# A graph network layer on one core: destinations broadcast instead of one-hot transposes, groups joined into sets, and one gathered tile of 25 copied column by column on ScalarE

## The chip, the cores and the metric

One core of a Trainium2 chip runs the whole program. The metric is the device time of one execution in microseconds, the median of three runs. A profile comes from one more execution; its times are measured from its first instruction.

## What is computed

Cut to what matters:

```python
h = relu(layernorm(x))                       # 12500 nodes x 128
s, d = src, dst                              # 400000 edges, sorted by dst
m = relu(concat([h[s], h[d], edge_attr]) @ w1 + b1) @ w2 + b2
agg = segment_sum(m, d, num_segments=12500)
# GRU cell: gates from agg @ w_ih + b_ih and h @ w_hh + b_hh
x_new = x + (1 - z) * n + z * h
```

The product with `w1` splits in three: `h[s] @ w1[0:128]` (called p), `h[d] @ w1[128:256]` (called q), and the edge attributes by the last 32 rows.

## The kernel before

**Setup.** The nodes are normalised in 14 batches; `hT` keeps h transposed in on-chip memory (128 features on the partitions, one node per column), and p is written to DRAM as `p_rows`, one row of 128 floats per node.

**Edges.** The 400000 edges are cut in 125 chunks of G = 5 groups of T = 5 tiles of P = 128 edges, so 25 tiles a chunk. `over_chunks` writes chunks 0 to 3 out, loops over the next ones and writes the last out again. Five engines run the same sequence, each with its own waits on semaphores.

- **GpSimd (POOL)** gathers `p_rows[src]` into `rows`, one indirect DMA for each tile (L423). It may overwrite a group's rows when `seg_ready` says that this group's sums of the chunk before are done.
- **VectorE (DVE)** builds the one-hot matrix of each tile's destinations against a window of W = 95 nodes (`build_onehot`, L790, 5 instructions a group), adds the products to the gathered rows (`add_pre`, L800), and adds the window sums to `acc` (`add_segments`, L809 and L810).
- **TensorE (PE)** transposes the one-hots (L1005), multiplies the window's features by `w1[128:256]` (L1008), forms q plus the edge part for five tiles (`pre_activation`, L1019), and sums messages per window node (`segment_sums`, L1032 and L1033).
- **ScalarE (ACT)** loads the window's base into a register (L563), copies the window's columns of `hT` to `h_win` (L568), copies the transposed one-hots to `lhs` with a count (`copy_onehot`, L574) and q to `rhs` (L575), and applies the ReLU to the rows (L580). Per chunk it also does the gate functions of 100 nodes (L592, L597) and issues a load and a store (L585, L601).
- **SyncE (SP)** loads indices and edge attributes.

The order on each engine is the order in which the code is written, shifted by groups with `before(c, s, back)`. The last chunk is followed by `finish_last`, which does the last 200 nodes' gates.

A group's step on ScalarE, for instance:

```python
copy_onehot(c, s)
if s + 1 < G:
    copy_window(c, s + 1)
old = before(c, s, 2)
if old:
    relu_message(*old)
```

Of the kernel before, what the change touches and what calls it, by code (L numbers as in the profile page):

```python
# [20 lines left out]
DST_PARTS = LOADS_AHEAD + 1  # L21
# [24 lines left out]
IOTA_PARTS = 5  # L46
assert W % IOTA_PARTS == 0

# [5 lines left out]

D = 128
# [3 lines left out]

def gnn_kernel(nc, x, src_cols, dst_cols, dst_rows, src_tiles, dst_tiles, ea_t, w1, b1, w2, b2, w_ih, b_ih, w_hh, b_hh, out):  # L60
    p_rows = nc.dram_tensor("p_rows", [NPAD, D], F32, kind="Internal").ap()
    base_f_dram = nc.dram_tensor("base_f_dram", [CHUNKS, G], F32, kind="Internal").ap()
    base_i_dram = nc.dram_tensor("base_i_dram", [CHUNKS, G], I32, kind="Internal").ap()
# [4 lines left out]
    with ExitStack() as ctx:  # L68
# [6 lines left out]
        def sems(name, n):  # L75
# [27 lines left out]
        base_i = low[ED:ED + 1, at:at + GROUPS].bitcast(I32)  # L103
        at += GROUPS
        assert at <= NPAD

        dst_int = sb("dst_int", [P, GROUPS * T], I32)
        dst_rel = dst_int[:, :].bitcast(F32)
        rows = sb("rows", [P, G, T, D])
        onehot = sb("onehot", [P, G, T, WB])  # L110
        base_bc = onehot[:, :, :, :].rearrange("p g t w -> p (g t w)")[:, 0:GROUPS]
        lhs = sb("lhs", [P, G, GE])
        rhs = sb("rhs", [P, G, D])
        h_win = sb("h_win", [P, W])
        w1_dst = sb("w1_dst", [P, D])
        idx = sb("idx", [P, G, T], I32)
        count = sb("count", [WB, G])
        ident = sb("ident", [P, P])
        iota_w = sb("iota_w", [P, IOTA_PARTS, W // IOTA_PARTS + 1])
# [15 lines left out]
        gmin = sb("gmin", [P, G])  # L135
        gmax = sb("gmax", [P, G])
        base_f = sb("base_f", [P, G])
        base_n = sb("base_n", [P, G], I32)
# [24 lines left out]
        g_b1, g_one = rhs[0:1, 0, :], lhs[0:1, 0, 0:P]  # L163
# [7 lines left out]
        onehotT_ps = ps[0:WB, 0:GE]  # L171
# [6 lines left out]
        q_ps = ps[0:W, GE:GE + D]  # L178
# [25 lines left out]
        dst_rel_ready, ones_set, acc_zeroed, deg_zeroed = (sem(n) for n in ("dst_rel_ready", "ones_set", "acc_zeroed", "deg_zeroed"))  # L204
        idx_in, ea_in, rows_in, h_win_ready = (sems(n, G) for n in ("idx_in", "ea_in", "rows_in", "h_win_ready"))
        onehot_ready, onehotT_ready, lhs_ready, pre_ready = (sems(n, G) for n in ("onehot_ready", "onehotT_ready", "lhs_ready", "pre_ready"))
        summed, message_ready, seg_ready, acc_added = (sems(n, G) for n in ("summed", "message_ready", "seg_ready", "acc_added"))
# [3 lines left out]
        fin_chain = sem("fin_chain")  # L211

# [3 lines left out]
        g_src_in, g_dst_in, g_ea_in = (sem(n) for n in ("g_src_in", "g_dst_in", "g_ea_in"))  # L216
        g_gathered = sems("g_gathered", 3)
        g_bc_ready, g_bcT_ready, g_pre_ready, g_summed, g_message_ready, g_seg_ready, g_new_ready = (sem(n) for n in (
            "g_bc_ready", "g_bcT_ready", "g_pre_ready", "g_summed", "g_message_ready", "g_seg_ready", "g_new_ready"))
# [14 lines left out]

        def over_chunks(eng, body, first=0):
            for c in range(first, LAG + 2):
                body(c)
            with eng.Fori(LAG + 2, CHUNKS) as c:  # L238
                body(c)


        def finishing(c):
            known = isinstance(c, int)
            return (c - LAG if not known or c >= LAG else None, c - LAG - 1 if not known or c > LAG else None)
# [17 lines left out]
        def _(sp):  # L262
# [24 lines left out]
            sp.dma_start(rhs[WB:P, :, :], w1[2 * D:2 * D + ED, :].unsqueeze(1).to_broadcast([ED, G, D])).then_inc(weights_in, 16)  # L287
            sp.dma_start(rhs[W:WB, :, :], b1.unsqueeze(0).unsqueeze(0).to_broadcast([1, G, D])).then_inc(weights_in, 16)
# [4 lines left out]
            sp.dma_start(dst_nat, dst_rows).then_inc(dstn_in, 16)  # L293
            turns = BATCHES // 2 - LOADS_AHEAD
# [14 lines left out]
            def load_indices(c, s):  # L309

                wait(sp, rows_in[s], c * (16 * T))
                sp.dma_start(idx[:, s, :], src_cols[bass.ds(c * (G * P) + s * P, P), :]).then_inc(idx_in[s], 16)
# [3 lines left out]

            part = GROUPS * T // DST_PARTS
            assert part * DST_PARTS == GROUPS * T

            def load_dst(k):  # L320
                sp.dma_start(dst_int[:, bass.ds(k * part, part)], dst_cols[:, bass.ds(k * part, part)]).then_inc(dst_in, 16)

            load_dst(0)
            with sp.Fori(turns, BATCHES // 2) as i:
                for par in range(2):
                    store(i, par)
                load_dst(i - (turns - 1))

            def load_group(c, s):

                if not (isinstance(c, int) and c == 0):
                    load_indices(c, s)

                wait(sp, pre_ready[s], c)
                sp.dma_start(lhs[WB:P, s, :], ea_t[:, bass.ds(c * (G * GE) + s * GE, GE)]).then_inc(ea_in[s], 16)

            def chunk(c):
                for s in range(G):
                    load_group(c, s)
                if isinstance(c, int) and c == 0:  # L340

                    sp.wait_ge(acc_zeroed, 2)
                    for par in range(2):
                        sp.wait_ge(p_stored[par], BATCHES // 2 * 16)
                        sp.wait_ge(hT_kept[par], BATCHES // 2)
                    sp.dma_start(deg[0:1, 0:N], acc[0:1, 0:N]).then_inc(deg_zeroed, 16)

            def general():

                for s in range(G):  # L350
                    sp.wait_ge(rows_in[s], 16 * T)
# [4 lines left out]
                with sp.Fori(0, TILES) as t:  # L356
# [4 lines left out]
                    sp.dma_start(lhs[WB:P, 0, 0:P], ea_t[:, bass.ds(t * P, P)]).then_inc(g_ea_in, 16)  # L361
# [9 lines left out]
            choose(sp, lambda: over_chunks(sp, chunk), general)  # L371

        @block.gpsimd
        def _(pool):
# [3 lines left out]
            nc.gpsimd.iota(iota_w[:, :, 0:W // IOTA_PARTS], [[W // IOTA_PARTS, IOTA_PARTS], [1, W // IOTA_PARTS]], base=0, channel_multiplier=0, allow_small_or_imprecise_dtypes=True)  # L378

            nc.gpsimd.iota(floor_c[:], [[1, 1]], base=-FN, channel_multiplier=FN, allow_small_or_imprecise_dtypes=True)  # L380
# [29 lines left out]
            def chunk(c):  # L410
# [5 lines left out]
                for s in range(G):  # L416
# [5 lines left out]
                    for t in range(T):  # L422
# [7 lines left out]
            def general():  # L430
                for s in range(G):
                    pool.wait_ge(rows_in[s], 16 * T)
# [34 lines left out]
        def _(act):  # L467
# [84 lines left out]
            act.dma_start(base_bc, base_f_dram.rearrange("(o c) g -> o (c g)", o=1).to_broadcast([P, GROUPS])).then_inc(base_bc_in, 16)  # L552
# [8 lines left out]
            def copy_window(c, s):  # L561

                b = act.value_load(base_i[0:1, bass.ds(c * G + s, 1)], min_val=0, max_val=BMAX)  # L563
                old = before(c, s, 1)
                if old:

                    act.wait_ge(onehotT_ready[old[1]], old[0] + 1)
                nc.scalar.copy(h_win[:], hT[:, bass.ds(b, W)]).then_inc(h_win_ready[s], 1)  # L568
# [612 lines left out]
```

## Time and profile before

| | us |
|---|---|
| median of 3 runs (4001.74 to 4002.7) | 4001.74 |
| the profiled execution | 4009.54 |
| its span, first to last instruction | 4007.8 |
| TensorE busy | 2996.9 (75%) |
| GpSimd busy | 2991.4 (75%) |
| VectorE busy | 1716.2 (43%) |
| ScalarE busy | 1281.7 (32%) |
| mean granted TensorE clock | 0.870 |

The profiled execution is 7.8 us longer than the median. Busy shares leave out what an engine's own sequencer does (register arithmetic, register loads, waits, DMA issues), so a low share does not by itself say that an engine has time to spare.

### The profile page before, as it was taken

What the parts mean: (1) busy time and instruction counts of PE and PEld (TensorE: products, weight loads), DVE (VectorE), ACT (ScalarE), POOL (GpSimd) and SP (SyncE); (2) the same over time, 40 slices, a digit from 0 to 9 for tenths busy, and PEclk for the clock granted to TensorE, in tenths of its full rate; (3) what the DMA queues carried; (4) which work ended last, traced back from release to release, by engine and by line L of the source; (5) the groups of instructions that cost most, each with busy time, mean ns of one, the idle gap of its engine ahead of it and who ended that gap; (6) DMA issues with size and microseconds to landing.
All of it is one profiled execution on the core that took longest, in us unless ns stands there. A gap on an engine that the chain in (4) does not pass through costs nothing.

```text
span 4007.8 us, 76313 instructions
## 1 busy us (share of the span) xinstructions
PE 2996.9 (75%) x20157; PEld 2691.1 (67%) x20157; DVE 1716.2 (43%) x6014; ACT 1281.7 (32%) x3575; POOL 2991.4 (75%) x3163
## 2 busy tenths in 40 slices
PE   5777777777777777777777777777777777777777
PEld 4667666667666666666666667666666666766666
DVE  6444444444444444444444444444444444444443
ACT  5333333333333323333333333333333333333332
POOL 4777777777777777777777777777777777777776
PEclk8888889888888888888888888888888888888887
DMA  6222222222222222222222222222222222222222
GB/s 187 68 69 69 69 69 69 69 69 70 69 69 69 70 70 69 69 69 70 69 69 69 69 69 70 69 69 69 70 69 69 69 69 69 69 69 69 69 69 56
DMA packets 275619, 287.99 MB, mean 72 GB/s; under 512 B 153847, under 2 KB 204696, under 8 KB 275475
## 3 DMA queue, kind: packets, MB, share of 16 engines
q0 software_dynamic: 100000, 205.00, 20.4%
q1 hardware_dynamic: 147282, 69.63, 6.1%
q10 hardware_dynamic: 28318, 13.14, 1.2%
q8 instruction: 8, 0.13, 0.0%
q14 instruction: 11, 0.09, 0.0%
HBM read 274.60 MB, written 12.83 MB: 72 GB/s over the span
## 4 chain that ended last, share of the span: by engine, by line
POOL 71%; issue 26%; DMA 1%; POOLq 1%; DVE 1%; PE 1%; ACT 0%; SPq 0%; DVEq 0%; ACTq 0%
POOL rows L423 71%; POOLq L227 1%; DMA p_rows<-low 1%; POOLq L238 0%; DMA acc<-in_x_dram 0%; DVE stats L700 0%; PE ps L1032 0%; PE ps L1005 0%; DVE mv L706 0%; DVE dst_int L779 0%; DMA onehot<-base_f_dram 0%; DVE low L725 0%; PE ps L1093 0%; PE ps L1094 0%; ACT low L505 0%
## 5 line engine op out<-in xcount | busy, mean ns | idle before, releaser
L423 POOL DMA_INDIRECT rows<-p_rows,idx x3125 | 2960.9, 947 | 964.4 <-issue 952.3
L574 ACT ACTIVATE lhs<-ps 96x640 f32<-96x640 f32 x625 | 437.6, 700 | 2590.5 <-PE ps L1008 2585.4
L1032 PE MATMUL ps<-onehot,rows 128*128 128x95 f32 x6250 | 915.1, 298 | 427.0 <-ACT rows L580 425.9
L1032 PEld LDWEIGHTS ps<-onehot,rows 128*128 128x128 f32 x6250 | 830.6, 210 | 520.9 <-ACT rows L580 290.4
L800 DVE TENSOR_TENSOR rows<-rows,ps 128x640 f32<-128x640 f32 x625 | 512.7, 820 | 1341.3 <-DMA rows<-p_rows,idx 1335.2
L1019 PE MATMUL ps<-rhs,lhs 128*128 128x128 f32 x6250 | 983.8, 315 | 68.9 <-DVE rows L800 68.4
L1019 PEld LDWEIGHTS ps<-rhs,lhs 128*128 128x128 f32 x6250 | 919.0, 229 | 97.2 <-issue 89.9
L1005 PE MATMUL ps<-ident,onehot 128*96 128x128 f32 x3125 | 547.6, 315 | 475.0 <-DVE onehot L790 473.8
L1005 PEld LDWEIGHTS ps<-ident,onehot 128*96 128x96 f32 x3125 | 385.6, 145 | 567.7 <-DVE onehot L790 560.2
L790 DVE TENSOR_SCALAR onehot<-iota_w,dst_int 128x95 f32<-128x95 f32 x3125 | 736.1, 298 | 51.1 <-issue 51.0
L580 ACT ACTIVATE rows<-rows 128x640 f32<-128x640 f32 x625 | 460.0, 736 | 84.6 <-DVE rows L800 82.1
L1008 PE MATMUL ps<-w_dst,h_win 128*95 128x128 f32 x1250 | 281.4, 313 | 0.0
L1008 PEld LDWEIGHTS ps<-w_dst,h_win 128*95 128x95 f32 x1250 | 208.2, 195 | 1.8
L809 DVE TENSOR_TENSOR acc<-acc,ps 128x95 f32 x625 | 158.5, 254 | 72.1 <-PE ps L1033 6.4
L1044 PE MATMUL ps<-low,b2ih 1*128 (+1 forms) x738 | 187.0, 336 | 0.0
L816 DVE SCALAR_TENSOR_TENSOR upd<-ps,bhh_col,rz 128x100 f32<-128x100 f32 x123 | 39.6, 322 | 317.0 <-ACT rz L592 317.0
L836 DVE TENSOR_TENSOR out_fin<-x_fin,ps 100x128 f32<-100x128 f32 x123 | 35.5, 289 | 320.8 <-PE ps L1051 320.8
L568 ACT COPY h_win<-hT 128x95 f32 x625 | 169.5, 271 | 5.2 <-issue 1.6
L1033 PE MATMUL ps<-ident,count 95*1 95x95 f32 x625 | 158.9, 254 | 0.0
L1043 PE MATMUL ps<-acc,w2ih 128*128 (+1 forms) x738 | 157.3, 298 | 0.0
L575 ACT COPY rhs<-ps 95x128 f32<-95x128 f32 x625 | 156.3, 250 | 0.0
L1044 PEld LDWEIGHTS ps<-low,b2ih 1*128 1x128 f32 x738 | 120.2, 203 | 40.6 <-issue 10.5
(94 smaller groups left out, 1307.9 us busy)
## 6 DMA issues: line engine op xcount, KB each, us to landing
rows<-p_rows,idx POOLq DMA_INDIRECT x3125
lhs<-in_ea_t_dram SPq DMA_DIRECT2D x625, 80.0 KB
idx<-in_src_cols_dram SPq DMA_DIRECT2D x625, 2.5 KB
p_rows<-low SPq DMA_DIRECT2D x14, 448.0 KB, 3.6
x_fin<-in_x_dram ACTq DMA_DIRECT2D x123, 50.0 KB
out_dram<-out_fin ACTq DMA_DIRECT2D x123, 50.0 KB
acc<-in_x_dram SPq DMA_DIRECT2D x13, 448.0 KB, 4.8
low<-in_dst_rows_dram SPq DMA_DIRECT2D x1, 1562.5 KB
```

The lines of the kernel that those rows point to most:

```text
L423: pool.indirect_dma_start(out=rows[:, s, t, :], out_offset=None, in_=p_rows[:, :], in_offset=bass.IndirectOffsetOnAxis(ap=idx[:, s, t:t + ...
L568: nc.scalar.copy(h_win[:], hT[:, bass.ds(b, W)]).then_inc(h_win_ready[s], 1)
L574: nc.scalar.activation(lhs[0:WB, s, :], onehotT_ps, ACT.Copy, accum_out=count[:, s:s + 1])
L580: nc.scalar.activation(m, m, ACT.Relu).then_inc(message_ready[s], 1)
L790: last = nc.vector.tensor_scalar(onehot[:, s, t, 0:W].rearrange("p (b a) -> p b a", b=W // IOTA_PARTS), iota_w[:, :, 0:W // IOTA_PARTS], d ...
L800: nc.vector.tensor_tensor(r, r, pre_ps[s % 2], ALU.add).then_inc(summed[s], 1)
L1005: nc.tensor.transpose(onehotT_ps[:, t * P:(t + 1) * P], onehot[:, s, t, :], ident[:])
L1008: nc.tensor.matmul(q_ps, h_win[:], w1_dst[:], start=True, stop=True).then_inc(onehotT_ready[s], 1)
L1019: last = nc.tensor.matmul(pre_ps[s % 2][:, t * D:(t + 1) * D], lhs[:, s, t * P:(t + 1) * P], rhs[:, s, :], start=True, stop=True)
L1032: nc.tensor.matmul(sg[:, 0:W], rows[:, s, t, :], onehot[:, s, t, 0:W], start=(t == 0), stop=(t == T - 1))
L1033: nc.tensor.transpose(sg[0:1, W:2 * W], count[0:W, s:s + 1], ident[0:W, 0:W]).then_inc(seg_ready[s], 1)
L1044: last = nc.tensor.matmul(gate_ps[:, g, :], b2ih[0:1, cols], d, start=False, stop=(g == 2))
```

## The change

**Destinations.** The one-hot transposes on TensorE and their copy by ScalarE go. Each group's 640 destinations are loaded by a DMA that repeats one DRAM row over 96 partitions (`dst_row`, 240 KB), and VectorE compares them with each partition's node number to give `lhs` and its counts (`build_lhs`). The other one-hot is built by one VectorE instruction for five tiles in place of five; its iota lies in PSUM.

**Sets.** Groups (0, 1, 2) and (3, 4) share a window base. A chunk has 2 windows, 2 q products, 2 additions to `acc` in place of 5 each.

**Stages.** The engines' steps are shifted further: a group's sums come three steps after its `lhs` (`AHEAD = 3`).

**One tile of 25.** The last tile of group 3 (`PICKED`) is not gathered. ScalarE reads its 128 source nodes into registers, 32 with one instruction, in four of the chunk's five steps, and copies for each the column `hT[:, node]` to a column of `picked`. TensorE multiplies `picked` by `w1[0:128]` into the same accumulator as that tile's pre-activation, and ScalarE's ReLU takes this tile from PSUM.

```diff
+PICKED = 3
+PICKS_ACT = (32, 32, 32, 32, 0)
+def gather_tiles(s):
+    return T - 1 if s == PICKED else T
...
-                    for t in range(T):
+                    for t in range(gather_tiles(s)):
                         pool.indirect_dma_start(
...
-            def copy_onehot(c, s):
-
-                act.wait_ge(onehotT_ready[s], c + 1)
-                wait(act, pre_ready[s], c)
-                nc.scalar.activation(lhs[0:WB, s, :], onehotT_ps, ACT.Copy, accum_out=count[:, s:s + 1])
-                nc.scalar.copy(rhs[0:W, s, :], q_ps).then_inc(lhs_ready[s], 1)
+            def load_picks(c, s):
+                if isinstance(c, int) and c == 0:
+                    act.wait_ge(pick_in, 32)
+                _, nodes = nc.values_load_multi_w_load_instructions(
+                    pick_act[s // 2][0:1, bass.ds(c * HALF + sum(PICKS_ACT[:s]) % HALF, PICKS_ACT[s])], (mybir.EngineType.Activation,),
+                    min_val=0, max_val=N - 1, skip_runtime_bounds_check_because=IN_RANGE)
+                return nodes
+            def pick_columns(c, s, nodes):
+                wait(act, pre_ready[PICKED], c)
+                for e, node in enumerate(nodes, sum(PICKS_ACT[:s])):
+                    last = nc.scalar.copy(picked[:, e:e + 1], hT[:, bass.ds(node, 1)])
+                last.then_inc(picked_act, 1)
...
+            def build_lhs(c, s):
+                dve.wait_ge(dst_row_in[s], c * 16 + 16)
+                wait(dve, pre_ready[s], c)
+                wait(dve, counted[SET_OF[s]], c)
+                nc.vector.tensor_scalar(lhs[0:W, s, :, 0:P], dst_row[0:W, s, :].rearrange("w (t p) -> w t p", t=T),
+                                        node_at[0:W, bass.ds(c * NSETS + SET_OF[s], 1)], 0.0, ALU.is_equal, ALU.add,
+                                        accum_out=count[0:W, s:s + 1]).then_inc(lhs_ready[s], 1)
...
+                    if not gathered:
+                        pe.wait_ge(picked_act, (c + 1) * sum(n > 0 for n in PICKS_ACT))
+                        last = nc.tensor.matmul(pre_ps[s % 2][:, t * D:(t + 1) * D], picked[:], w1_keep[:], start=False, stop=True)
...
+                segment_sums(c, G - 3)
                 segment_sums(c, G - 2)
-
-                pe.wait_ge(lhs_ready[G - 1], CHUNKS)
+                back(CHUNKS - LAG - 1)
+
+                pe.wait_ge(rhs_ready[NSETS - 1], CHUNKS)
                 pe.wait_ge(summed[G - 2], CHUNKS)
+                pe.wait_ge(summed[G - 1], CHUNKS)
+                pe.wait_ge(onehot_ready[G - 1], CHUNKS)
```

ScalarE inside the loop over chunks, before: one group's step (an ISA row is one fused register instruction of the sequencer).

```order
L574 ACTIVATE lhs,count<-ps 96x640 [waits pre_ready1,onehotT_ready1]
L575 COPY rhs<-ps 95x128
L563 ISA
L563 TENSOR_LOAD low
L563 ISA x2
L568 ISA [waits onehotT_ready1]
L568 COPY h_win<-hT 128x95
L580 ACTIVATE rows<-rows 128x640 [waits summed4]
```

The same engine after the change, the step of group 3: a set's q and window, the ReLU of group 1, and the start of the picks.

```order
L639 COPY rhs<-ps 95x128 [waits pre_ready4,q_ready1]
L627 ISA
L627 TENSOR_LOAD low
L633 ISA [waits q_ready1]
L633 COPY h_win<-hT 128x95
L659 ACTIVATE rows<-rows 128x640 [waits summed1]
L644 ISA
L644 TENSOR_LOAD low
L653 ISA [waits pre_ready3]
L653 COPY picked<-hT 128x1
L653 ISA
L653 COPY picked<-hT 128x1
```

The pair of ISA and COPY stands 32 times after each such load, so 128 times a chunk; the loop's body has some 290 rows on this engine in place of some 50. The transposed one-hots' copy is gone from every step.

GpSimd in the loop after the change, groups 2 to 4 of the chunk (before, every group had one row and then x4).

```order
L487 DMA rows<-p_rows,idx 128x128 [waits seg_ready2,idx_in2,p_stored1]
L487 DMA rows<-p_rows,idx 128x128 x4
L487 DMA rows<-p_rows,idx 128x128 [waits seg_ready3,idx_in3,p_stored1]
L487 DMA rows<-p_rows,idx 128x128 x3
L487 DMA rows<-p_rows,idx 128x128 [waits seg_ready4,idx_in4,p_stored1]
L487 DMA rows<-p_rows,idx 128x128 x4
```

One gather of 25 is gone; what GpSimd waits for is the same.

## Rows read from the trace of the kernel before

**Rows 1.** Page, part 1: busy time, share, instructions.
```profile
PE 2996.9 (75%) x20157; PEld 2691.1 (67%) x20157; DVE 1716.2 (43%) x6014; ACT 1281.7 (32%) x3575; POOL 2991.4 (75%) x3163
```
**Rows 2.** Page, part 4: the chain that ended last.
```profile
POOL 71%; issue 26%; DMA 1%; POOLq 1%; DVE 1%; PE 1%; ACT 0%; SPq 0%; DVEq 0%; ACTq 0%
```
**Rows 3.** Groups by line on GpSimd: busy, mean ns, idle before, releasers.
```profile
L423 POOL DMA_INDIRECT rows<-p_rows,idx x3125 | 2960.9, 947 | 964.4 <-issue 952.3 <-DMA p_rows<-low 11.7 <-PE ps L1033 0.3
```
**Rows 4.** Timeline of GpSimd: first gather, sixth, two in mid-run, the last.
```profile
76.12 1.13 POOL L423 DMA_INDIRECT rows<-p_rows,idx  x1 [11.73 <-DMA p_rows<-low]
...
85.34 0.95 POOL L423 DMA_INDIRECT rows<-p_rows,idx  x1 [0.30 <-issue]
...
2001.33 0.94 POOL L423 DMA_INDIRECT rows<-p_rows,idx  x1 [0.31 <-issue]
2002.58 0.95 POOL L423 DMA_INDIRECT rows<-p_rows,idx  x1 [0.30 <-issue]
...
3988.77 0.94 POOL L423 DMA_INDIRECT rows<-p_rows,idx  x1 [0.30 <-issue]
```
**Rows 5.** Timeline of ScalarE in mid-run: start, length.
```profile
2002.55 0.19 ACT L574 ACTIVATION_READ_ACCUMULATOR lhs<-ps 96x1 f32 x1
2002.64 0.25 ACT L575 COPY rhs<-ps 95x128 f32<-95x128 f32 x1
2002.85 0.27 ACT L568 COPY h_win<-hT 128x95 f32 x1
2003.03 0.73 ACT L580 ACTIVATE rows<-rows 128x640 f32<-128x640 f32 x1
2003.67 0.56 ACT L592 ACTIVATE rz<-ps,brz_col 128x100 f32<-128x100 f32 x2
...
2009.26 0.36 ACT L597 ACTIVATE cand<-cand,bih_col 128x100 f32<-128x100 f32 x1
...
2021.26 0.55 ACTq L601 DMA_DIRECT2D out_dram<-out_fin  x1
```
**Rows 6.** Lines 563, 568, 803: sequencer instructions, ns min/median/max.
```profile
L563 ACTq TENSOR_LOAD <-low x625: 272/287/822, 85.8 to 3974.3; - x157
L568 ACTq FUSED_REGOPS  x625: 37/43/48, 86.4 to 3975.0; - x157
L803 DVEq TENSOR_LOAD <-low x625: 299/305/318, 96.5 to 3992.3; - x157
```
**Rows 7.** Line 790 between 2011.0 and 2012.2 us: first and last start.
```profile
L790 DVEq FUSED_REGOPS  x5: 57/57/64, 2011.0 to 2011.5; - x5
```
**Rows 8.** Groups by line on VectorE.
```profile
L790 DVE TENSOR_SCALAR onehot<-iota_w,dst_int 128x95 f32<-128x95 f32 x3125 | 736.1, 298 | 51.1 <-issue 51.0
L800 DVE TENSOR_TENSOR rows<-rows,ps 128x640 f32<-128x640 f32 x625 | 512.7, 820 | 1341.3 <-DMA rows<-p_rows,idx 1335.2 <-PE ps L1019 5.6
```
**Rows 9.** Timeline of TensorE: ten products each.
```profile
3976.16 1.35 PE L1032 MATMUL ps<-onehot,rows 128*128 128x95 f32 x10 [0.87 <-ACT rows L580]
3979.11 1.28 PE L1019 MATMUL ps<-rhs,lhs 128*128 128x128 f32 x10
3986.87 2.45 PE L1032 MATMUL ps<-onehot,rows 128*128 128x95 f32 x10 [3.20 <-ACT rows L580]
```
**Rows 10.** Stretches: PE, PEld, DVE, ACT, POOL busy, granted clock, DMA share, GB/s.
```profile
2000.00:2313.00 313.00, 237.44 (x1591) 213.23 (x1589) 133.32 (x460) 98.22 (x280) 236.68 (x251) 0.87 0.27 69
```
**Rows 11.** Page, part 3: queues of instruction fetches.
```profile
q8 instruction: 8, 0.13, 0.0%
q14 instruction: 11, 0.09, 0.0%
```
**Rows 12.** Timeline of the end: the last group's rows, sums and gates.
```profile
3989.27 1.60 PE L1085 MATMUL ps<-hT,whh_sb 128*128 128x200 f32 x4
3990.66 0.87 PE L1086 MATMUL ps<-hT,whh_sb 128*128 128x200 f32 x2
3991.34 0.82 DVE L800 TENSOR_TENSOR rows<-rows,ps 128x640 f32<-128x640 f32 x1 [4.88 <-DMA rows<-p_rows,idx]
3992.99 2.45 PE L1032 MATMUL ps<-onehot,rows 128*128 128x95 f32 x10 [1.46 <-ACT rows L580]
4005.47 0.31 ACTq L641 DMA_DIRECT2D out_dram<-rows  x1
```

More of the change, by code:

```diff
@@ L53 @@
 LN = LAG * FN
+SETS = ((0, 1, 2), (3, 4))
+NSETS = len(SETS)
+SET_OF = {s: k for k, members in enumerate(SETS) for s in members}
+STARTS = {members[0]: k for k, members in enumerate(SETS)}
+ENDS = {members[-1]: k for k, members in enumerate(SETS)}
+ONEHOT_PLACE = (0, 1, 2, 0, 1)
+AHEAD = 3
+PGAP = P + 4
+PICKED = 3
+PICKS_ACT = (32, 32, 32, 32, 0)
+N_ACT = sum(PICKS_ACT)
+assert N_ACT == P
+IN_RANGE = "src holds node indices, 0 to N - 1"
+BASE_IN_RANGE = "the window's base is a least node index, and a minimum holds it at BMAX"
 D = 128
@@ L232, in before, with after, exists, onehot_holder @@
             return None if isinstance(c, int) and c2 < 0 else (c2, s2)
+        def after(c, s, ahead):
+            return (c, s + ahead) if s + ahead < G else (c + 1, s + ahead - G)
+        def exists(group):
+            return group is not None and not (isinstance(group[0], int) and group[0] >= CHUNKS)
+        def onehot_holder(c, s):
+            return before(c, s, next(b for b in range(1, G + 1) if ONEHOT_PLACE[(s - b) % G] == ONEHOT_PLACE[s]))
+        def set_before(c, k):
+            c2, k2 = (c, k - 1) if k else (c - 1, NSETS - 1)
+            return None if isinstance(c, int) and c2 < 0 else (c2, k2)
         def over_chunks(eng, body, first=0):
@@ L237, in over_chunks @@
                 body(c)
[L238 removed]
+            with eng.Fori(LAG + 2, CHUNKS - 1) as c:
                 body(c)
+            body(CHUNKS - 1)
         def finishing(c):
             known = isinstance(c, int)
[L244 removed]
+            return (c - LAG if not known or LAG <= c < CHUNKS else None, c - LAG - 1 if not known or c > LAG else None)
         def over_fin(eng, body):
@@ L334, in load_group @@
                 wait(sp, pre_ready[s], c)
-                sp.dma_start(lhs[WB:P, s, :], ea_t[:, bass.ds(c * (G * GE) + s * GE, GE)]).then_inc(ea_in[s], 16)
+                sp.dma_start(lhs[WB:P, s, :, 0:P],
+                             ea_t[:, bass.ds(c * (G * GE) + s * GE, GE)].rearrange("f (t p) -> f t p", t=T)).then_inc(ea_in[s], 16)
             def chunk(c):
                 for s in range(G):
[L339 to L346, printed above, removed]
+                    ahead = after(c, s, AHEAD)
+                    if exists(ahead):
+                        if not (isinstance(ahead[0], int) and ahead[0] == 0):
+                            load_indices(*ahead)
+                        load_group(*ahead)
+                    if s == 2 and exists((c + 1, 0)):
+                        load_destinations(c + 1)
@@ new lines, in fast @@
+            def fast():
+                load_destinations(0)
+                for s in range(AHEAD):
+                    load_group(0, s)
+                sp.wait_ge(acc_zeroed, 2)
+                for par in range(2):
+                    sp.wait_ge(p_stored[par], BATCHES // 2 * 16)
+                    sp.wait_ge(hT_kept[par], BATCHES // 2)
+                sp.dma_start(deg[0:1, 0:N], acc[0:1, 0:N]).then_inc(deg_zeroed, 16)
+                sp.wait_ge(ranges_ready, 1)
+                sp.wait_ge(w2ih_copied, 2)
+                tile = PICKED * T + T - 1
+                nodes = src_tiles.rearrange("(c k) p -> k c p", k=G * T)[tile:tile + 1, :, :]
+                for k, row in enumerate(pick_act):
+                    sp.dma_start(row.rearrange("o (c e) -> o c e", e=HALF), nodes[:, :, k * HALF:(k + 1) * HALF]).then_inc(pick_in, 16)
+                over_chunks(sp, chunk)
@@ L644, in fast @@
             def fast():
+                copy_window(0, 0)
                 over_chunks(act, chunk)
-                for back in (2, 1):
-                    relu_message(CHUNKS - 1, G - back)
-                store(CHUNKS - LAG - 1)
+                relu_message(CHUNKS - 1, G - 2)
+                relu_message(CHUNKS - 1, G - 1)
+                n = CHUNKS - LAG - 1
+                load_x_fin(n)
+                gate_activations(n)
+                candidate(n)
+                store(n)
                 finish_last()
```

362 lines of the change are left out of this document (214 added, 148 removed).

## The prediction

> **What bounds the kernel now.** I read the shares first, and they mislead: TensorE and GpSimd are both busy 75% [rows 1]. The chain that ended last settles it: 71% GpSimd and 26% "issue", almost nothing of TensorE [rows 2]. The group of gathers shows where the "issue" is: 964 us of idle time before the 3125 gathers, 952 of it released by nothing but the issue itself, 0.3 us by a product of TensorE [rows 3]. So GpSimd is full although the page says 75%: a gather takes 0.95 us and the next starts 0.30 us later. From the sixth gather at 85.34 to the last at 3988.77 there are 3119 intervals in 3903.43 us, 1.2515 us each [rows 4]. A chunk of 25 takes 31.29 us. The rest of the span, 4007.8 - 3125 x 1.2515 = 97 us, is setup and end. The other engines follow the gathers: VectorE's additions wait 1335 us for rows to land [rows 8].
>
> **What the change takes off that path.** 125 of 3125 gathers go: 125 x 1.2515 = 156.4 us, if nothing else becomes the pace. GpSimd's own waits stay as they are: `seg_ready` of the same group a chunk earlier, some four groups (24 us) after that group's rows landed. A chunk then has 24 x 1.2515 = 30.04 us, and every other engine has to fit in that.
>
> **ScalarE, the engine that gets the work.** It loses the transposed one-hots' copy and gets 128 copies of one column, each behind a fused register instruction, and four loads of 32 registers. No row shows a copy of one column in a series, so I bound it.
> - The engine's side: an instruction of one column is 0.19 us long, and the next starts 0.09 us after it, so neighbours overlap [rows 5]. The window copy of 95 columns gives the same: its successor starts 0.18 us later, 0.08 of which are the columns.
> - The sequencer's side: VectorE issues pairs of the same kind. Five register instructions start in 0.5 us, so about 0.13 us for a pair [rows 7]. VectorE's register instruction takes 57 ns and ScalarE's 43 [rows 6, 7]; by that ratio a pair costs ScalarE 0.10 us.
>
> I take 0.10 us, as both sides agree: 128 x 0.10 = 12.8 us a chunk. The upper end is the whole length, 0.19.
>
> The rest of ScalarE's chunk from [rows 5, 6]: five ReLUs at a spacing of 0.64, 3.2 us; two window copies (0.18) and two q copies (0.21), 0.8; the gates 0.56 and the candidate 0.36, 0.9; two DMA issues of 0.55, 1.1; the two windows' register loads with their neighbours, about 0.4 each, 0.8; about 0.4 for the loop's branch and what lies between. Together 20.0 us.
>
> That leaves 10.0 us for four loads, 2.5 us each. A load of one register takes 0.287 us [rows 6]. What one of 32 takes no row shows. The lower end is one trip for all of them, 0.3; the upper end is a trip for each. VectorE's sequencer is slower by 57/43, yet its load takes 305 ns and not 380 [rows 6], so only some 55 ns of a load go with the sequencer and about 0.23 us are the trip to memory; 32 trips would be 7.4 us. The load has no effect under 0.07 us for each further register, and eats the whole gain at 0.08 to 0.09. I take the lower end, nearest to the row there is, with 4 x 0.4 = 1.5 us: ScalarE has 21.5 us of work in 30.04. This is the least certain step.
>
> Order matters little then. A turn with picks is 0.64 + 3.2 + 0.4, some 4.3 us, against a group's 5.0 or 6.3 us of gathers, so the ReLU of the next group is not held up. The picks of four turns must be done before group 3's product; behind that product stand group 1's sums, for which GpSimd asks some 15 us later.
>
> **The others.** VectorE: the five one-hot instructions of a group (5 x 0.236 = 1.18) become one of 475 columns, by the 640 columns of `add_pre` (0.82) at most 0.65 [rows 8]. The new compare of 640 columns with a count is at most 0.82 + 0.19. So 1.65 in place of 1.18 a group, 2.4 us more a chunk; three additions to `acc` fewer give about 1 us back. From 43% it goes to about 15 us in 30. TensorE loses 25 transposes and three q products: five groups of 1.28 + 1.35 us and about 3 us of the rest [rows 9], 16 us in 30. If less work made the clock fall for good, sums at 2.45 us [rows 9] and products in proportion would need about 28 us, still under 30.04. It is now granted 0.87 [rows 10]. The DMA engines carry 69 GB/s at a share of 0.27 [rows 10]; 1.2 MB more a chunk is 40 GB/s, so about 0.43. Rows land later, which five buffers cover. ScalarE's loop body grows to some 290 rows; only 19 packets of instructions are in the whole trace [rows 11], so I have no price for code that no longer stays on chip, and 8.5 us a chunk on ScalarE to hide it in.
>
> **Start and end.** The first gather waits for the last store of p [rows 4], which the change doesn't touch. At the end the last rows are added at 3991.34, and the sums begin 1.65 us later, as the 2.4 us of products with `whh` were done before [rows 12]. After the change TensorE waits for that addition and the last one-hot, and behind them for `back` of chunk 122, before it does them: 0.82 + 0.65 for VectorE, about 2.5 for the two `acc` additions with their load, candidate, tanh, update and transpose, then 2.4 of products. Sums begin about 7 us after the rows, 5.3 later than now.
>
> **Sum.** For the profiled execution 4009.5 - 156.4 + 5.3 = 3858.4. It lies 7.8 above the median of the runs shown, so the median becomes 4001.7 - 156.4 + 5.3 = **3851 us**, 3.8% less.
>
> **Rivals.**
> - *A trip for each register.* ScalarE's chunk is 20.0 + 4 x 7.4 = 49.7 us, GpSimd waits for sums, and the time is 125 x 49.7 + 97 + 5 = 6310 us. For it: the trip of 0.23 us is most of the one load that the trace shows [rows 6]. Against it: nothing in the trace. The Trainium skill, "Runtime: NRT & Kernel Launch", section "Instruction fetch mechanics", speaks for it: a register load costs about 200 ns a register even in bulk. By that figure ScalarE would need 20.0 + 25.6 us a chunk and the kernel 5800 us, an estimate from that page; no row here shows a load of more than one register. I give this 14%, with every price of a register that ends above 4230 us.
> - *One-column copies don't overlap.* Then 128 x 0.19 = 24.3, and ScalarE has 24.3 + 7.2 + 1.5 = 33.0 us a chunk: 125 x 33.0 + 102 - 8 = 4220 us. It decides from 0.167 us a copy (30.04 - 8.7 over 128), and makes the kernel slower than before from 0.176. Against it are the starts 0.09 us apart [rows 5]. The Trainium skill, "Advanced Engine Details and Errata", section "The Read-Write Bubble", says that memory accesses are pipelined within an instruction but not between instructions on ScalarE; the trace shows an overlap of 0.1 us all the same. Register prices of 0.09 to 0.13 us end in the same place. Together 8%.
> - *ScalarE nearly full, or a wait once a chunk* (the load at 2.5 us, a code fetch, a late ReLU): each us over 30.04 costs 125 us and still leaves a gain of up to 1.25 us a chunk: 3876 to 3993 us, 8%. A chunk of just 31.3 us would be no change, 2%.
> - The forecast: 68%.
>
> **How the numbers follow.** The likeliest case alone spans 3842 (no loss at the end) to 3876. With the partial gain and the first slow case the range is 3842 to 4230, which leaves out 18%. About 0.2% (8 us) is what a measurement can tell from no change. Faster: 0.68 + 0.08 = 0.76; same 0.02; slower 0.14 + 0.08 = 0.22.
>
> **What would show it.** Right: 3000 gathers still 1.25 us apart with "issue" as releaser, the chain of waits still GpSimd's; the picks' copies starting 0.10 us apart; the four loads well under 2.5 us; ScalarE idle before its ReLUs, waiting for VectorE's sums. Wrong: gathers at a group's start waiting for TensorE's sums, those for ScalarE's picks, and ScalarE never idle; the load's own length then tells the first rival from the second. If the gathers' spacing itself grew, the added DMA traffic would be the cause.

## The result

The changed kernel takes 3948.97 us (median of 4 runs, 3946.32 to 3953.04); the kernel before took 4001.74 us beside it (4000.62 to 4002.7). The ratio is 0.9869 with a 95% interval of 0.9856 to 0.9881: 1.3% faster, where 3.8% was forecast. The time lies in the range, and in what the prediction called its third rival, a wait once a chunk (3876 to 3993 us).

The page of the changed kernel: busy times, queues of instruction fetches, and the chain that ended last.

```profile
span 3946.7 us, 93036 instructions
...
PE 2953.6 (75%) x16157; PEld 2688.7 (68%) x16157; DVE 1742.8 (44%) x4517; ACT 2270.3 (58%) x17700; POOL 2861.4 (73%) x3039
...
q14 instruction: 618, 5.06, 0.4%
q8 instruction: 8, 0.13, 0.0%
...
PE 38%; ACT 26%; issue 17%; ACTq 13%; DVE 3%; DVEq 1%; DMA 0%; SPq 0%
ACT picked L653 23%; PE ps L1175 12%; ACTq L644 11%; PE ps L1156 7%; PE ps L1190 6%; PE ps L1192 4%; PE ps L1189 4%; DVE rows L918 3%; PE ps L1160 2%; PE ps L1193 2%; ACT cand L679 1%; ACTq L653 1%; ACTq L627 1%; ACT rhs L639 1%; DVE low L930 0%
```

The chain had been 71% GpSimd [rows 2]. Now no line of GpSimd is among its parts: the picks (L653), their register loads (L644) and TensorE's products are. The busy shares of TensorE, VectorE and GpSimd hardly moved against [rows 1], so it is again the chain that tells, not the shares. The queue that fetches code (q14) carried 618 packets instead of 11 [rows 11].

The groups by line of the gathers and of VectorE's addition of the rows, and then who waited for whom (us in total, times, longest):

```profile
L487 POOL DMA_INDIRECT rows<-p_rows,idx x3000 | 2831.0, 944 | 1022.4 <-issue 871.5 <-PE ps L1178 110.5 <-PE ps L1175 29.4
L918 DVE TENSOR_TENSOR rows<-rows,ps 128x640 f32<-128x640 f32 x625 | 492.8, 788 | 633.5 <-PE ps L1160 561.6
```
```profile
PE ps L1160 <- ACT picked L653: 371.6, 125, 3.8
ACT rows L659 <- DVE rows L918: 365.7, 129, 8.9
ACT rhs L639 <- issue: 345.2, 119, 3.7
POOL rows L487 <- PE ps L1178: 110.5, 89, 1.4
DVE rows L918 <- DMA rows<-p_rows,idx: 39.2, 16, 3.8
```

GpSimd now waits for TensorE: 89 times for the sums of a set (L1178), 1.24 us each where a plain step is 0.30. VectorE waited 1335 us for rows to land [rows 8]; now it waits 39 us for them and 562 us for the product with the picked columns (L1160). TensorE waits for the picks, and ScalarE's ReLU (L659) for VectorE's rows, 2.9 us a chunk: each waits for another, and GpSimd for one of them. The row with L639 is the end of ScalarE's loop, where it stands still for 2.9 us (345.2 / 119) without waiting for another engine. GpSimd's timeline shows where it waits (start, length; idle before and releaser in brackets):

```profile
76.02 1.12 POOL L487 DMA_INDIRECT rows<-p_rows,idx  x1 [11.02 <-DMA p_rows<-low]
115.71 0.94 POOL L487 DMA_INDIRECT rows<-p_rows,idx  x1 [9.86 <-PE ps L1175]
126.23 0.94 POOL L487 DMA_INDIRECT rows<-p_rows,idx  x1 [4.60 <-PE ps L1175]
...
2033.33 0.94 POOL L487 DMA_INDIRECT rows<-p_rows,idx  x1 [0.30 <-issue]
2034.58 0.94 POOL L487 DMA_INDIRECT rows<-p_rows,idx  x1 [0.31 <-issue]
...
2058.06 0.94 POOL L487 DMA_INDIRECT rows<-p_rows,idx  x1 [1.31 <-PE ps L1178]
...
3917.45 0.94 POOL L487 DMA_INDIRECT rows<-p_rows,idx  x1 [0.30 <-issue]
```

Apart from these waits the gathers are as close as before (1.25 us), so the traffic added doesn't slow them. The lost time is in three places. In the opening, chunk 1's first two groups wait 9.86 and 4.60 us, 13.9 over the plain 0.30. From 115.71 to the last gather there are 2975 intervals of 1.249 us and the opening's second wait of 4.3; of the 3801.7 us that leaves 82, 0.67 us in each of the 123 chunks after, all of it at the first gather of group 2. At the end 29.25 us follow the last gather's start against 19.03 before (4007.8 - 3988.77, [rows 4]): 10.2 more, 5.3 forecast. Beyond the forecast that is 13.9 + 82 + 4.9 (10.2 less the 5.3 that it had) = 101 us, and the median missed the forecast by 98.

### The profile page after: what moved, and what is told of

It is laid out like the page before. It is cut to its first block, busy times and chain, and to the rows that moved or that the text cites. A ratio compares the mean times of both kernels' runs of the same rounds, so it can differ in the third digit from the quotient of the medians.

```text
span 3946.7 us, 93036 instructions
## 1 busy us (share of the span) xinstructions
PE 2953.6 (75%) x16157; PEld 2688.7 (68%) x16157; DVE 1742.8 (44%) x4517; ACT 2270.3 (58%) x17700; POOL 2861.4 (73%) x3039
## 3 DMA queue, kind: packets, MB, share of 16 engines
q14 instruction: 618, 5.06, 0.4%
## 4 chain that ended last, share of the span: by engine, by line
PE 38%; ACT 26%; issue 17%; ACTq 13%; DVE 3%; DVEq 1%; DMA 0%; SPq 0%
ACT picked L653 23%; PE ps L1175 12%; ACTq L644 11%; PE ps L1156 7%; PE ps L1190 6%; PE ps L1192 4%; PE ps L1189 4%; DVE rows L918 3%; PE ps L1160 2%; PE ps L1193 2%; ACT cand L679 1%; ACTq L653 1%; ACTq L627 1%; ACT rhs L639 1%; DVE low L930 0%
## 5 line engine op out<-in xcount | busy, mean ns | idle before, releaser
L487 POOL DMA_INDIRECT rows<-p_rows,idx x3000 | 2831.0, 944 | 1022.4 <-issue 871.5
L653 ACT COPY picked<-hT 128x1 f32 x16000 | 1568.0, 187 | 805.9 <-issue 805.5
L1175 PE MATMUL ps<-onehot,rows 128*128 128x95 f32 x6250 | 1087.9, 339 | 102.6 <-DVE low L930 98.9
L1175 PEld LDWEIGHTS ps<-onehot,rows 128*128 128x128 f32 x6250 | 1045.0, 256 | 140.9 <-issue 140.9
L1156 PE MATMUL ps<-rhs,lhs 128*128 128x128 f32 x6250 | 1107.5, 342 | 5.3 <-DVE lhs L901 3.1
L659 ACT ACTIVATE rows<-rows 128x640 f32<-128x640 f32 x625 | 443.9, 710 | 406.3 <-DVE rows L918 365.7
L901 DVE TENSOR_SCALAR_CACHE_REDUCE lhs<-dst_row,node_at 95x640 f32<-95x640 int32 x625 | 542.5, 868 | 8.9 <-DMA dst_row<-in_dst_rows_dram 8.9
L892 DVE TENSOR_TENSOR onehot<-dst_rel,ps 128x475 f32<-128x475 f32 x625 | 399.6, 639 | 0.0
L1160 PE MATMUL ps<-w_keep,picked 128*128 128x128 f32 x250 | 89.6, 456 | 371.6 <-ACT picked L653 371.6
L1160 PEld LDWEIGHTS ps<-w_keep,picked 128*128 128x128 f32 x250 | 56.0, 279 | 408.3 <-ACT picked L653 408.3
L1140 PE MATMUL ps<-w_dst,h_win 128*95 128x128 f32 x500 | 126.6, 342 | 230.5 <-ACT h_win L633 230.5
L639 ACT COPY rhs<-ps 95x128 f32<-95x128 f32 x250 | 64.5, 258 | 346.0 <-issue 345.2
L1140 PEld LDWEIGHTS ps<-w_dst,h_win 128*95 128x95 f32 x500 | 78.5, 195 | 254.8 <-ACT h_win L633 228.8
L1189 PEld LDWEIGHTS ps<-acc,w2ih 128*128 128x128 f32 x738 | 195.3, 323 | 0.0
```

The costliest lines, as they stand in the source:

```text
L487: pool.indirect_dma_start(out=rows[:, s, t, :], out_offset=None, in_=p_rows[:, :], in_offset=bass.IndirectOffsetOnAxis(ap=idx[:, s, t:t + ...
L653: last = nc.scalar.copy(picked[:, e:e + 1], hT[:, bass.ds(node, 1)])
L659: nc.scalar.activation(m, m, ACT.Relu).then_inc(message_ready[s], 1)
L892: nc.vector.tensor_tensor(onehot[:, ONEHOT_PLACE[s], :, 0:W], dst_rel[:, s * T:(s + 1) * T].unsqueeze(2).to_broadcast([P, T, W]), iota_ps. ...
L901: nc.vector.tensor_scalar(lhs[0:W, s, :, 0:P], dst_row[0:W, s, :].rearrange("w (t p) -> w t p", t=T), node_at[0:W, bass.ds(c * NSETS + SET ...
L1156: last = nc.tensor.matmul(pre_ps[s % 2][:, t * D:(t + 1) * D], lhs[:, s, t, 0:P], rhs[:, k, :], start=True, stop=gathered)
```

## The experiments

**1. Which engine's share of the 0.67 us?** The suspects were the register loads of the picks' indices (theory L), the code fetches at ScalarE's loop end (F), and TensorE's gate products (T).

One register a load, all other instructions kept. It leaves out the right choice of columns:

```diff
-  pick_act[s // 2][0:1, bass.ds(c * HALF + sum(PICKS_ACT[:s]) % HALF, PICKS_ACT[s])]
+  pick_act[s // 2][0:1, bass.ds(c * HALF + sum(PICKS_ACT[:s]) % HALF, 1)]
-  for e, node in enumerate(nodes, sum(PICKS_ACT[:s])):
+  for e, node in enumerate([nodes[0] + k for k in range(PICKS_ACT[s])], sum(PICKS_ACT[:s])):
```

> Each of the four loads takes one register instead of 32, and the 32 copies of its turn take the 32 columns behind that one index, so the product takes other columns than the edges' own; every other instruction of every engine is the same, in number and order. Theory L (the load of 32 registers, 2.14 us against one register's 0.28 to 0.46, is what makes the chunk 30.7 us instead of 30.0): ScalarE loses some 7 us a chunk, the first gather of group 2 no longer waits, the chunk falls to 30.0 us: 120 x 0.7 = 84 us less, and a few more of the opening: 3850 to 3870 us. Theory F (the instruction fetches of a loop body of about 290 instructions, 2.8 us at the loop's end): nothing of it is changed, 3935 to 3950 us, and the wait at group 2 stays. Theory T (TensorE's gate products at a low clock ahead of the sums of group 2): the same as F.

Measured: 3853.07 us (ratio 0.9626, 0.961 to 0.9642), inside theory L's interval. The next kernel keeps the load of one register and shortens the loop body as well, from some 290 instructions to some 170, as all copies of a turn share one address (it leaves out the right columns too):

```diff
-  for e, node in enumerate(nodes, sum(PICKS_ACT[:s])):
+  for e, node in enumerate(nodes * PICKS_ACT[s], sum(PICKS_ACT[:s])):
```

> As the kernel with one register a load, but all 32 copies of a turn read the one column (the product takes other columns than the edges' own), so that the 31 further address computations fall away and the loop body is half as long. Theory L: the pace is GpSimd's already with one register a load, so this one is within 5 us of it. Theory F: only here the time falls, to 3850 to 3880 us, the hole at the loop's end shrinks from 2.8 us to under 1, and the instruction queue carries half the packets. If the copies are held up by the address computation, their spacing falls from 93 ns; if by the copy itself, it stays.

Measured: 3849.56 us (0.9622, 0.9606 to 0.9638), within 4 us of the other. The loads, by line (ns min/median/max), of the changed kernel, of one register, and (L646) of the kernel of experiment 3 with two loads of 16:

```profile
L644 ACTq TENSOR_LOAD <-low x500: 1964/2143/2172, 101.5 to 3912.3; - x167
```
```profile
L644 ACTq TENSOR_LOAD <-low x500: 281/455/475, 99.9 to 3816.5; - x167
```
```profile
L646 ACTq TENSOR_LOAD <-low x1000: 1013/1028/1216, 100.6 to 3913.8; - x167
```

One register takes 0.455 us here, 16 take 1.03, 32 take 2.14: (2.143 - 0.455) / 31 = 0.054 us for each further one on average, less of it up to 16 (0.04) than beyond (0.07). The Trainium skill, "Runtime: NRT & Kernel Launch", section "Instruction fetch mechanics", has about 200 ns a register even in bulk. That page of the Trainium skill speaks of loads from HBM; these are from on-chip memory, and the rows give about a quarter of its figure.

Code fetching was tested only weakly: in the first kernel it was untouched, with 618 packets, and the gain was there all the same. In the second the fetches fell to 17 packets and no more than 4 us came of it. A turn of its picks in the timeline, and 31 picks of the changed kernel:

```profile
2008.76 3.07 ACT L653 COPY picked<-hT 128x1 f32 x32
```
```profile
2021.74 2.97 ACT L653 COPY picked<-hT 128x1 f32 x31 [0.21 <-issue]
```

With the last copy's 0.19 us taken off that is 31 and 30 intervals of 0.093 us, the same without an address computation between them as with one: the address computation doesn't set the spacing.

**2. The same work, moved.** On ScalarE the load ahead of the ReLU:

```diff
+  picking = exists((c, s)) and PICKS_ACT[s]
+  nodes = load_picks(c, s) if picking else None
   if old:
       relu_message(*old)
-  if exists((c, s)) and PICKS_ACT[s]:
-      pick_columns(c, s, load_picks(c, s))
+  if picking:
+      pick_columns(c, s, nodes)
```

> The same work as the changed kernel; in each step of ScalarE the load of the 32 registers stands ahead of the ReLU instead of behind it. Theory L: ScalarE waits about 1.9 us at the ReLU of group 4 for VectorE, and the load now lies under that wait: one 2.14 us load leaves the circle that is 0.7 us too long, so the wait of GpSimd goes or nearly goes: 3865 to 3890 us. Theory F: the load was not what held it, 3935 to 3955 us. Slower than 3955 us if the ReLUs, now 2 us later where the rows are already there, hold TensorE more than the picks did.

Measured: 3860.89 us (0.9646, 0.963 to 0.9662), the whole loss and 4 us under the interval, which had left some of it. On TensorE the gate products into the wait for the picks:

```diff
+  if s == 4 and n is not None:
+      pe.wait_ge(acc_added[NSETS - 1], c * 2)
+      gates(n)
   if old:
       pre_activation(*old)
   if s != 1 and older:
       segment_sums(*older)
-  if s == 4 and n is not None:
-      pe.wait_ge(acc_added[NSETS - 1], c * 2)
-      gates(n)
```

> The same work as the changed kernel; TensorE's nine gate products (about 5.3 us at the low clock) stand ahead of the edge products of group 3, where TensorE waits 2.6 to 3 us for the picked columns, instead of behind the sums of group 1. Theory T: with the picks' wait filled, the sums of group 2 come 2.5 to 3 us earlier, GpSimd's wait at group 2 goes, and the chunk is 30.0 us: 3860 to 3880 us. Theories L and F in their strict form (ScalarE alone sets 30.7 us): no change, 3940 to 3955 us. If the circle runs through both engines, either edit alone ends the wait.

Measured: 3856.11 us (0.9637, 0.9621 to 0.9653), 4 us under theory T's interval, with ScalarE's loads as long as ever (2.13 us). So L and T each account for the whole loss, which a single full engine can't do. It is a circle through several engines: work whose result comes back, an engine at a time, to where it began a chunk later. Any cut in it serves. The gathers of this kernel:

```profile
L487 POOL DMA_INDIRECT rows<-p_rows,idx x3000 | 2831.1, 944 | 939.5 <-issue 896.9 <-PE ps L1175 21.2 <-DMA p_rows<-low 11.0
```

The wait for L1178 has gone from the group's line. What is left of waiting for TensorE is the opening (10.33 and 4.78 us), and 20.4 us follow the last gather's start (3833.70 of 3854.1).

The circle can be read off the changed kernel's chain of waits, one chunk of it (start us, us, what):

```profile
1996.92 0.81 DVE rows L918
1997.75 0.06 ACT rows L659
1997.84 2.15 ACTq L644
...
2008.48 0.22 ACT rhs L639
...
2014.37 0.44 ACT picked L653 x4
2014.85 0.49 PE ps L1160 x2
2015.34 1.09 PE ps L1175 x10
2016.43 0.35 PE ps L1189 x2
...
2021.02 0.68 PE ps L1193 x2
2021.69 2.18 PE ps L1156 x10
2023.87 2.08 PE ps L1175 x10
2025.95 0.17 PE ps L1178
...
2026.36 0.07 DVE acc L929
...
2026.70 0.81 DVE rows L918
...
2044.63 0.79 PE ps L1160 x2
2045.42 2.08 PE ps L1175 x10
```

From the rows of group 4 on VectorE (1996.92) to the same a chunk later (2026.70): ReLU 4, then the loads and picks of turns 1, 2 and 3 on ScalarE (turn 0 is the first 32 columns of a chunk, turn 3 the last 32; 17.1 us), then on TensorE the product with the picks, group 1's sums, the gates (2016.43 to 2021.69), group 4's edge products and group 2's sums (11.3 us), then the two adds ahead of the rows. It is 29.78 us in this round, just under the 29.98 of 24 gathers. In the next round the same ten sums after the picks take 2.08 us instead of 1.09, and it is 31.15 us.

The whole trace has the same pattern: the rows of group 4 start at 2026.69, 2057.84, 2088.88, 2119.78 and 2149.56 us, so 31.15, 31.04, 30.90 and 29.78 apart, and so on. Of the 120 rounds from the fourth to the last but one, 30 take 29.7 to 29.8 us and the others 30.8 to 31.2, 30.7 on average. ScalarE's part does not vary (17.9 us from the addition's start to the product with the picks). TensorE's part does; here it is for four rounds, the second figure the length, the one behind the last bracket the granted clock (0.50 is 1.2 GHz throughout, 1.00 would be 2.4):

```profile
2014.85:2026.11 11.26, 11.26 (x51) 9.80 (x51) 1.25 (x2) 5.59 (x39) 8.52 (x10) 0.57 0.40 102
2044.63:2057.25 12.62, 12.62 (x51) 11.17 (x51) 1.25 (x2) 5.58 (x39) 9.38 (x10) 0.50 0.36 95
2106.80:2119.14 12.34, 12.33 (x51) 11.08 (x51) 1.25 (x2) 5.60 (x39) 9.23 (x10) 0.51 0.38 97
2137.68:2148.95 11.27, 11.22 (x51) 9.80 (x51) 1.25 (x2) 5.63 (x39) 8.53 (x10) 0.57 0.41 102
```

TensorE waited for the picks before each, 2.6 to 3.5 us in these four. Where its clock is still at the higher level for some 1.5 us of the stretch (0.57), the circle fits; where nearly all of the stretch is at the lower level, the same work takes 1.1 to 1.4 us more and the circle is too long. So by these rows the loads made the circle as long as the chunk, and TensorE's lower clock carried it over.

**3. Is the staging itself worth anything, and the loop's end?** Four more kernels. The change without its on-chip tile (all 25 tiles gathered):

```diff
-PICKED = 3
-PICKS_ACT = (32, 32, 32, 32, 0)
+PICKED = None
+PICKS_ACT = (0, 0, 0, 0, 0)
```

> The rest of the change without its on-chip tile: the staged pipeline, the sums by sets and the broadcast destinations stay, but all 25 tiles of a chunk are gathered, and there are no picked columns, loads of their indices or second product. If the 24 gathers are the whole of the gain, GpSimd paces at 25 x 1.25 = 31.25 us a chunk, and the time is that of the kernel with the gate products first (3856 us) plus 125 x 1.25 = 156 us: 4005 to 4020 us, the kernel before within 0.4%. Rival: the new staging gains or loses by itself (its opening and its end), under 3990 or over 4030 us.

Measured: 3999.26 us, ratio 0.9995 (0.9985 to 1.0004), 6 us under the interval expected and no difference from before. So the rest of the change, taken together, neither costs nor brings anything, and the gathers left out are all of the gain. From here to the kernel with the gates first are 143 us: the 156 of the gathers, less some 14 that the picks cost in the opening (10.33 and 4.78 us there; with all tiles gathered none waits over the plain 0.30 after the first). Two chunks to a turn of ScalarE's loop:

```diff
-  over_chunks(act, chunk)
+  for c in range(LAG + 2):
+      chunk(c)
+  with act.Fori((LAG + 2) // 2, (CHUNKS - 1) // 2) as pair:
+      chunk(pair * 2)
+      chunk(pair * 2 + 1)
+  chunk(CHUNKS - 1)
```

> The same work as the changed kernel; only ScalarE's loop is written with two chunks to a turn, so that its loop ends 60 times instead of 120, in a body of twice the length. Theory of the circle, with the stop of 2.8 us at the loop's end on it: a stop less in every second chunk takes 1.4 us a chunk from a circle that is 0.69 us too long: 3860 to 3900 us. Rival: the fetches of the longer body cost the same wherever they fall, or the stop lies where ScalarE would wait anyway: 3935 to 3955 us.

Measured: 3947.15 us (0.9864, 0.9848 to 0.9881): no change, the rival held and the circle as I had drawn it (loop end included) fell. Its waits, against the changed kernel's 345.2 and 365.7 us above:

```profile
ACT rhs L639 <- issue: 164.3, 59, 3.5
ACT rows L659 <- DVE rows L923: 534.6, 192, 8.8
```

The stop came 59 times instead of 119, and of the 181 us saved 169 came back as waiting for VectorE's rows. Splitting the loads shows the same.

```diff
-  _, nodes = nc.values_load_multi_w_load_instructions(... 32 registers ...)
+  nodes, part = [], PICKS_ACT[s] // 2
+  for k in range(2):
+      nodes += nc.values_load_multi_w_load_instructions(... part registers from k * part ...)[1]
```

> The same work as the changed kernel; each load of 32 registers is two loads of 16. By a fixed part and a price per register (0.455 us for one register, 2.143 us for 32, so 0.054 us for each further one) a load of 16 takes 1.27 us and the two of a turn 2.54 us: 0.4 us a turn, 1.6 us a chunk on ScalarE, and as it sits on a circle that is already too long, up to 120 x 1.6 = 190 us more: 4060 to 4145 us. If the price were one of the instruction and not of its registers, each takes 2.1 us and the chunk grows by 8.6 us, to some 4900 us.

Measured: 3951.76 us (0.9875, 0.9856 to 0.9895, 2 runs), the changed kernel's time. That is 108 us under the interval. Two loads of 16 take 2.06 us, not 2.54, so the load's price was expected too high, and this kernel does not test it. By accident the loop's code was no longer fetched anew (23 packets instead of 618, though the loop has instructions more; why, I did not settle), and the stop at the loop's end went too. The changed kernel's ScalarE around it, then the same place with split loads (whose lines stand 3 lower in the file from the loads on, as in all kernels that load in parts or move VectorE's rows):

```profile
2018.32 0.26 ACT L639 COPY rhs<-ps 95x128 f32<-95x128 f32 x1 [2.88 <-issue]
...
2027.53 0.74 ACT L659 ACTIVATE rows<-rows 128x640 f32<-128x640 f32 x1 [1.90 <-DVE rows L918]
```
```profile
2015.00 0.26 ACT L639 COPY rhs<-ps 95x128 f32<-95x128 f32 x1 [0.30 <-issue]
...
2028.17 0.74 ACT L662 ACTIVATE rows<-rows 128x640 f32<-128x640 f32 x1 [4.85 <-DVE rows L921]
```

The 2.6 us saved at the loop's end come back in this chunk as 2.95 us more of waiting before ReLU 4, for VectorE. The loop's end and turn 0 lie in the part of ScalarE's chunk that has room; the circle takes in only what follows ReLU 4. Theory F is out. The last of the four has both moves of experiment 2:

> The same work as the changed kernel, with the load ahead of the ReLU on ScalarE and the gate products ahead of the edge products of group 3 on TensorE. The circle is open twice, so GpSimd paces as with either edit alone: 3848 to 3862 us, within 0.3% of them. If the edits still had something of the circle to share out in the first chunks, up to 10 us less than the better one; if the loads ahead delay the ReLUs of a TensorE that now runs early, 3865 us or more.

Measured: 3860.33 us (0.9649, 0.9633 to 0.9665), within its interval and as either alone.

**4. Three forecasts from the circle.** On VectorE, in step 1, `add_pre(c - 1, 4)` ahead of `add_segments(c - 1, 0)`:

```diff
-  add_segments(done[0], ENDS[done[1]])
+  if s != 1:
+      add_segments(done[0], ENDS[done[1]])
   old = before(c, s, 2)
   if s == 1 and old:
       add_pre(*old)
+  if s == 1 and done:
+      add_segments(done[0], ENDS[done[1]])
```

> The same work as the changed kernel; on VectorE, in step 1, the rows of group 4 are added ahead of the sums of group 2 instead of behind them. Theory of the circle (picks of turns 1 to 3 on ScalarE, product with the picked columns, sums of group 1, gates, edge products of group 4 and sums of group 2 on TensorE, the adds and the rows of group 4 on VectorE, ReLU of group 4 on ScalarE, and again turn 1): the sums of group 2 (2.1 us) and the two adds (0.7 us) leave the circle, which has 0.67 us too much; the wait of GpSimd goes, 3855 to 3870 us. Rival, that ScalarE's total of work sets 30.65 us: no change, 3940 to 3955 us.

Measured: 3859.94 us (0.9646, 0.963 to 0.9662), within the circle's interval. A third engine's order, and the same result. Then the same 128 picks, shared out otherwise over the turns:

```diff
-PICKS_ACT = (32, 32, 32, 32, 0)
+PICKS_ACT = (40, 24, 32, 32, 0)
```

> The same work as the changed kernel; the 128 columns are shared out over the turns as 40, 24, 32, 32 in place of 32 each (the first turn's indices by a load of 32 and one of 8). Theory of the circle: turn 0 is not on it and turn 1 is; there 8 copies at 0.093 us and 8 registers at 0.07 us less are 1.3 us, more than the 0.67 us too much: the chunk falls to 30.0 us, 3855 to 3870 us. Rival, that ScalarE's total sets the pace: it grows by 0.2 us, 3945 to 3975 us.

And the reverse, `(24, 40, 32, 32, 0)`; a turn of 40 loads its indices in parts of 32 and 8.

> The reverse: 24, 40, 32, 32 (turn 1's indices by a load of 32 and one of 8). Theory of the circle: turn 1 gets 8 copies (0.74 us) and a load of 8 registers more (0.6 to 0.75 us), all on the circle: 1.35 to 1.5 us in each of some 120 chunks, 160 to 180 us more than the changed kernel, 4110 to 4130 us and so slower than the kernel before. Rival, that ScalarE's total sets the pace: 3945 to 3975 us, as for the other order.

Measured: 3872.39 us (0.9677, 0.9661 to 0.9694) and 4116.24 us (1.029, 1.0273 to 1.0307). Sixteen columns in turn 1 instead of turn 0 turn a gain into a loss against before, with the same number of picks, registers and loads. That the engine's total sets the pace is refuted. The first of them is 2 us over its interval and 16 us behind the kernel with the gates first. Who waited for whom with 40 in turn 0 (L1178 there is the sums' product, L1175 in the changed kernel):

```profile
ACT rows L662 <- DVE rows L921: 90.1, 141, 8.5
POOL rows L487 <- PE ps L1178: 42.8, 81, 13.1
```

ScalarE waits only 0.7 us a chunk for rows now, against 2.9 in the changed kernel, so its own work is nearly the whole chunk: ahead of turn 0's picks its two loads leave it idle for 3.8 us, where one load leaves 1.6. And the opening's wait is longer (13.1 us at most, against 9.9). How its 16 us divide between the two is not settled. In the other direction GpSimd's waits for the sums of a set (L1181; L1178 in the changed kernel) were:

```profile
POOL rows L487 <- PE ps L1181: 277.7, 117, 3.0
```

117 waits of 2.37 us, less 0.30 each, are 242 us, where the changed kernel has 89 x 0.94 = 84: 158 us more, where the two profiled executions are 161 apart (4109.11 against 3948.5; the medians 167).

## Why the forecast was wrong, step by step

- **What bounds the kernel, and what a gather less brings: right.** 3000 gathers at 1.249 us. With the circle cut (gates first) 3856 us were measured, 5 over the forecast's 3851. That it is so near is partly luck: in that kernel the opening cost 14.5 us that the sum hadn't, the end cost 3.9 us less than it had, and that some 5.5 us more were saved no run explains.
- **ScalarE's copies at 0.10 us: right**, 0.093; they overlap, being 0.187 us long.
- **The loads of 32 registers at 0.4 us: mis-sized by a factor of five**, 2.14 us, so 8.6 us a chunk instead of 1.5. This is the term that the prediction called its least certain. It is necessary for the loss: with one register a load the loss is gone.
- **"The load has no effect under 0.07 us for each further register" and "Order matters little then": the step that failed.** By its own test (under 2.5 us a load) the forecast should have held at 2.14 us, since 20.0 + 8.6 = 28.6 us fit in 30.04, and ScalarE's total did fit: it still waited 2.9 us a chunk for rows. The test was the wrong one. It held each engine's total against the chunk, and checked the order only of ReLU and picks, and of group 1's sums. It did not follow what stands on TensorE behind the product with the picks: the gates and group 4's products, then group 2's sums, and from there VectorE's queue to ReLU 4, behind which turn 1 stands on ScalarE. Round that circle three loads count, and the chunk takes 30.65 us on average instead of 29.98. With the clock as it was, it would take 0.67 / 3 = 0.22 us less a load, so 1.92 us or 0.047 us for each further register, to bring it to 29.98: an estimate from these rows, and below the 0.054 that was measured.
- **TensorE at 16 to 28 us in 30, hence harmless: wrong for the same reason.** Its total fits, but 11.3 us of it lie on the circle, with the gates among them; out of the circle they cost nothing (3856.11 us). It priced the lower clock for TensorE's total (28 us) and not for this stretch, where the lower level in three rounds of four makes the difference between 29.8 and 31 us.
- **Code no longer on chip: foreseen as a risk without a price, and free here.** ScalarE's loop stops 2.9 us at its end, with 618 packets of code. The Trainium skill, "Runtime: NRT & Kernel Launch", section "Instruction fetch mechanics", says that a taken branch out of the current window of code stalls until the target page has been fetched; this trace agrees. What decides whether a loop meets it the runs leave open: the kernel with split loads has the longer body and 23 packets. Here it fell where ScalarE has room.
- **The opening: left out.** The forecast had nothing for it, and 13.9 us were lost. About half of it is the loads again: with one register a load the two waits are 5.93 and 1.81 us, 7.1 together over the plain step. The other half was not tested.
- **The end, 5.3 us: for a kernel in step too much** (20.4 us with gates first, 1.4 over before), **for this one too little** (10.2), since the gates and group 4's products still stood behind the last picks.
- **The other rivals.** Loads at a trip each (6310 us) and copies that don't overlap (4220 us) both failed. The third rival had the right form and size, a wait once a chunk, with a chance of 8% and no mechanism worked out.
- **The signs.** Gathers at a group's start waited for TensorE's sums and TensorE for the picks, as the prediction said of a wrong forecast. "ScalarE never idle" was not seen, and that is what tells the circle from a full engine.

The best version is the change with the gate products first: 3856.11 us, ratio 0.9637.

## What to carry to other kernels

An engine whose work fits in the period can still set it: follow each result round to the next turn of the same instruction, over every in-order queue that it passes, and add up that circle at the durations of the lower clock. Where work is put on a circle, first look for what in it could stand in somebody's wait; a move of nine products gave back 93 us here without any work less. And where one price is unknown, work out how high it may be from the circle, not from the engine's total.

## What the runs showed of the hardware

- A register load from on-chip memory holds ScalarE's queue for 0.455 us with one register (medians; the shortest 0.281), 1.03 with 16 and 2.14 with 32.
- Copies of one column are 0.187 us long and start 0.093 us apart, with or without an address computation in between. The prediction set against that the Trainium skill, "Advanced Engine Details and Errata", section "The Read-Write Bubble", by which memory accesses are not pipelined between instructions on ScalarE. The rows show recorded lengths that overlap by half; whether part of the 0.093 us is the latency that the section speaks of they don't show.
- A loop body with about 290 ScalarE instructions was fetched anew in every turn, with some 5 packets of 8 KB (618, 5.06 MB) and a stop of 2.9 us; one of some 170 was not (17 packets), and neither was one with split loads, which is longer than the first (23).
- The same stretch of TensorE's work (the product with the picks, two groups' sums, the gates, one group's edge products) takes 11.3 us where the granted clock is 0.57 and 12.6 where it is 0.50.
- The profiled execution of the kernel before had its gathers 1.2515 us apart [rows 4], that of the changed kernel 1.249. Over 3125 gathers that is 7.8 us, the amount by which the former stood above its median; that its other executions had the shorter spacing is not shown, as none of them was profiled.
